# Six bound registers set once for 316 indirect transfers of GpSimd

## The chip, the core and the metric

The kernel runs on one core of a Trainium2 chip. A core has TensorE for matrix products (PE in the profile), VectorE (DVE), ScalarE (ACT), GpSimd (POOL) and SyncE (SP). Each engine has its own list of instructions; semaphores order them against each other. An engine has a sequencer in front of it, which works off the list; what the sequencer does by itself (set a register, wait on a semaphore, issue a DMA) stands in the profile under the engine's name with a q, as POOLq. The metric is the device time of one execution in microseconds. One execution was also recorded by the hardware profiler.

## The reference, cut to what matters

4096 tokens of width 128 pass through six layers. The first and third are a mixture of 8 experts, the fourth and sixth one of 16 experts with a limited capacity, the second is a convolution with attention-like cumulative products and a dense layer, and the fifth is a linear recurrence.

```
x = x + 0.5 * moe8(layernorm(x))                 # argmax of the scores chooses one of 8 experts per token
x = x + attn(layernorm(x))                       # conv, q/k/v, two cumulative sums, gelu layer
x = x + 0.5 * moe8(layernorm(x))
x = x + 0.5 * moe16(layernorm(x))                # one of 16 experts per token, at most 320 tokens each
x = x + recurrence(layernorm(x))                 # state = a * state + u_b, then layernorm
x = x + 0.5 * moe16(layernorm(x))
```

A mixture computes only the chosen expert, so tokens have to be brought together by expert and sent back to their places afterwards. That is what the indirect transfers do.

## The kernel before, in words

All tokens stay in the tile X: 32 tiles of 128 tokens, handled as 8 chunks of 4 tiles. Every engine works through an order written out by hand (TABLE), a list of steps with a number, and each step is one branch of that engine's program. Waits are on semaphores that count finished steps. A wait is attached to the instruction that follows it on its engine; where a step has several waits, instructions of their own (EVENT_SEMAPHORE, line 268) take all but the last.

The steps of GpSimd are these:

- `send.n` (line 1281) scatters tile n of X, whole rows of 132 numbers, to the DRAM array `xs`, to row numbers that VectorE has put into IDX. There are 128 of them, 32 for each mixture. In the 8-expert layers they come in groups (the first 8 or 20 tiles, then the rest), in the 16-expert layers one chunk after another. A group's first send waits for the array's fill and the row numbers in an instruction of its own, and then for `pnm`, which is VectorE's last step on the rows.
- `home.t` (line 1295) scatters the result tile `yt` of tile t of sorted tokens back to the tokens' places in the DRAM array `y`. There are 92, 46 for each 8-expert layer. It waits for `ty`, the step of VectorE that writes `yt`, and from the sixth on, in an instruction of its own, for the landing of the transfer five before.
- `ehome.i` (line 1310) does the same for one of the 16 experts in three blocks (128, 128 and 64 tokens), 96 transfers in all. The first and the third block wait for `eout`, VectorE's step at line 1065. In the last layer it writes to `out`, and its last block is the last work of the program.
- `ppow`, `apow`, `rpow` (lines 1261 and 1279) are small powers, 63 TENSOR_TENSOR instructions, for the layer norms.

SyncE loads sorted tiles (`tload`, line 500), experts' weights, and after the last `home` of a group the results (`yload`, line 515) back into X. The next layer needs them.

Each indirect transfer is issued through `send` (line 1263) or `home` (line 1267). Rows whose number is above a bound are dropped. The bound is given as a plain number, and the language then puts a register move (MOVE) ahead of the transfer; that MOVE is the instruction that follows the wait, so the step's last wait stands on it.

Of the kernel before, what the change touches and what calls it, by code (L numbers as in the profile page):

```python
# [14 lines left out]
P = 128  # L15
NT = 32
# [5 lines left out]
E0, E1 = 8, 16  # L22
# [8 lines left out]
ROOM = [T0[nt] for nt in GNT]  # L31
# [5 lines left out]
REACH = NT * P  # L37
# [242 lines left out]
def build(nc, x, consts, rows, cols, mats, xt, w01, w02, w1x, out):  # L280
    ctx = ExitStack()
    with ctx:
        sems = {}

        def sem(name):
            if name not in sems:
                sems[name] = ctx.enter_context(nc.semaphore("s_" + name))
            return sems[name]
# [10 lines left out]
        def dram(name, nrows, width):  # L299
            return nc.dram_tensor(name, (nrows, width), F32, kind="Internal").ap()  # L300
# [78 lines left out]
        xs0 = [dram(f"xs0_{g}", ROOM[g] * P, ROW) for g in range(4)]  # L379
        xs1 = [dram(f"xs1_{m}", E1 * REACH, ROW) for m in range(2)]  # L380
# [24 lines left out]
        def batch_x(b, col):  # L405

            c, n = BATCH[b][0] % NC, len(BATCH[b])
            return X[:, c * CT:(c + n) * CT, col]
# [29 lines left out]
        def wait_home(lane, t):  # L438
            lane.wait_ge(sem(f"home{t % NHS}"), turns(t, NHS))
# [15 lines left out]
        def filled0(g):  # L455
            return 32 if ROOM[g] >= ZR else 16
# [800 lines left out]
        def pool_program():  # L1257
            e = POOL.eng

            def power(dst, src):  # L1260
                return e.tensor_tensor(dst, src, MH[:, 0:dst.shape[1]], ALU.pow)  # L1261

            def send(dst, hi, n):
                return e.indirect_dma_start(dst, bass.IndirectOffsetOnAxis(ap=IDX[:, n:n + 1], axis=0), X[:, n, :], None,  # L1264
                                            bounds_check=hi, oob_is_err=False)

            def home(dst, src, ix):
                return e.indirect_dma_start(dst, bass.IndirectOffsetOnAxis(ap=ix, axis=0), src, None,  # L1268
                                            bounds_check=NT * P - 1, oob_is_err=False)

            e.memset(MH[:, :], -0.5).then_inc(sem("half"), 1)
            for b in PAD:
                e.memset(b[:, :, 0:3], 0.0).then_inc(sem("pad"), 1)
            POOL.wait_ge(sem("half"), 1)
            for stage, i in ORDER["pool"]:
                if stage == "ppow":
                    n = len(BATCH[i]) * CT
                    POOL.wait_ge(sem("peps"), i + 1)
                    e.tensor_tensor(batch_x(i, R_R), SMP[i % NSM][:, 0:n], MH[:, 0:n], ALU.pow).then_inc(sem("ppow"), 1)  # L1279
                elif stage == "send":  # L1280
                    p, n = divmod(i, NT)
                    c = n // CT
                    POOL.wait_ge(sem("pnm"), BOF[p * NC + c] + 1)
                    if p < 2:
                        g = 2 * p + (c >= FIRST[p])
                        POOL.wait_ge(sem("rsel"), 2 * (g + 1))
                        POOL.wait_ge(sem(f"fill{g}"), filled0(g))
                        send(xs0[g], ROOM[g] * P - 1, n).then_inc(sem(f"sent{g % 2}"), 16)
                    else:
                        k = (p - 2) * NC + c  # L1290
                        POOL.wait_ge(sem("q3"), 2 * (k + 1))
                        POOL.wait_ge(sem("q2"), 2 * (k + 1))
                        POOL.wait_ge(sem(f"fill{p + 2}"), 16 * E1)
                        send(xs1[p - 2], E1 * REACH - 1, n).then_inc(sem("sentx"), 16)
                elif stage == "home":
                    POOL.wait_ge(sem("ty"), i + 1)
                    if i >= NHS:
                        wait_home(POOL, i - NHS)
                    yt = YT[i % NYT]
                    home(y[i >= TILE0[2]], yt[:, :], XI[i % NXI][:, R_ID:ROW].bitcast(U32)).then_inc(sem(f"home{i % NHS}"), 16)  # L1300
                elif stage == "apow1":
                    POOL.wait_ge(sem("astat1"), 4 * (i + 1))
                    power(SMA[0][i % NA][:, 4:12], SMA[0][i % NA][:, 16:24]).then_inc(sem("apow1"), 1)
                elif stage == "apow2":
                    POOL.wait_ge(sem("astat2"), 3 * (i + 1))
                    power(SMA[1][i % NA][:, 4:8], SMA[1][i % NA][:, 16:20]).then_inc(sem("apow2"), 1)
                elif stage == "apow3":
                    POOL.wait_ge(sem("astat3"), 3 * (i + 1))
                    power(SMA[2][i % NA][:, 4:8], SMA[2][i % NA][:, 16:20]).then_inc(sem("apow3"), 1)
                elif stage == "ehome":  # L1310
                    xe, ye = XE[i % NXE], YE[i % NYE]
                    if i >= E1:
                        POOL.wait_ge(sem("out"), 16 * NC)
                    for b, (o, n) in enumerate(BL):
                        POOL.wait_ge(sem("eout"), 2 * i + (2 if b == 2 else 1))
                        home(y[1] if i < E1 else out, ye[0:n, b, :], xe[0:n, b, R_ID:ROW].bitcast(U32)).then_inc(sem(f"ye{i % NYE}"), 16)
                elif stage == "rpow":
                    POOL.wait_ge(sem("rstat"), 3 * (i + 1))
                    power(SMA[0][i % NA][:, 4:8], SMA[0][i % NA][:, 16:20]).then_inc(sem("rpow"), 1)
                elif stage == "rpow2":  # L1320
                    POOL.wait_ge(sem("rve"), i + 1)
                    power(SMA[1][i % NA][:, 4:8], SMA[1][i % NA][:, 16:20]).then_inc(sem("rpow2"), 1)
# [3 lines left out]
        dve_program()  # L1326
        act_program()
        pool_program()


# [60 lines left out]
```

## Time and profile before

| | before |
|---|---|
| median of 3 runs | 739.43 us (738.84 to 741.69) |
| the profiled execution | 738.26 us |
| its span, first to last instruction | 737.0 us |
| mean granted TensorE clock | 0.905 of full speed |
| PE, DVE, ACT, POOL busy | 81%, 59%, 45%, 53% of the span |

The span's stages: about 20 us of loading and routing, the first 8-expert layer to about 156 us, the second layer to about 256 us, the second 8-expert layer to about 420 us, the fourth layer with its 16 experts to about 550 us, the recurrence to about 640 us, and the last mixture of 16 experts to the end. In a profile a busy share is an average over such stages, and what a change is worth is read from the chain of waits in the stage where it acts. The chain goes back from the last instruction to whatever released each one.

### The profile page before, as it was taken

What the parts mean: (1) busy time and instruction counts of PE and PEld (TensorE: products, weight loads), DVE (VectorE), ACT (ScalarE), POOL (GpSimd) and SP (SyncE); (2) the same over time, 40 slices, a digit from 0 to 9 for tenths busy, and PEclk for the clock granted to TensorE, in tenths of its full rate; (3) what the DMA queues carried; (4) which work ended last, traced back from release to release, by engine and by line L of the source; (5) the groups of instructions that cost most, each with busy time, mean ns of one, the idle gap of its engine ahead of it and who ended that gap; (6) DMA issues with size and microseconds to landing.
All of it is one profiled execution on the core that took longest, in us unless ns stands there. A gap on an engine that the chain in (4) does not pass through costs nothing.

```text
span 737.0 us, 13471 instructions
## 1 busy us (share of the span) xinstructions
PE 597.7 (81%) x3640; PEld 487.9 (66%) x3640; DVE 433.2 (59%) x1670; ACT 332.0 (45%) x989; POOL 388.4 (53%) x386
## 2 busy tenths in 40 slices
PE   5568889988999967999999442999956866199996
PEld 5568889966757934899899341676734755066774
DVE  5554566569996687475568360455538897135453
ACT  1135366529577335445468532343306633334330
POOL 1667754446113185147757783355554488425555
PEclk9999899998999999999999855999986876599998
DMA  8676674660034222356684153377433122325410
GB/s 320 265 216 171 172 199 135 178 181 4 15 156 104 56 87 60 80 148 192 180 261 134 53 185 81 106 203 202 139 95 111 58 64 84 77 75 156 119 43 13
DMA packets 75257, 95.39 MB, mean 129 GB/s; under 512 B 12658, under 2 KB 51481, under 8 KB 74928
## 3 DMA queue, kind: packets, MB, share of 16 engines
q1 hardware_dynamic: 63664, 75.77, 35.4%
q0 software_dynamic: 10112, 14.55, 6.0%
q10 hardware_dynamic: 1408, 4.21, 1.7%
q8 instruction: 31, 0.51, 0.3%
q14 instruction: 42, 0.34, 0.1%
HBM read 66.24 MB, written 33.64 MB: 136 GB/s over the span
## 4 chain that ended last, share of the span: by engine, by line
PE 60%; DVE 11%; POOL 9%; issue 9%; DMA 8%; ACT 2%; SPq 0%; DVEq 0%; POOLq 0%; ACTq 0%
PE ps L704 10%; PE ps L639 9%; PE ps L711 9%; PE ps L631 9%; POOL xs L1264 6%; PE ps L686 3%; PE ps L679 3%; PE ps L588 3%; PE ps L549 3%; PE ps L653 3%; DMA X<-y 2%; PE ps L694 2%; DMA y<-yt,xi 2%; PE ps L718 2%; DMA xs<-X,IDX 1%
## 5 line engine op out<-in xcount | busy, mean ns | idle before, releaser
L1264 POOL DMA_INDIRECT xs<-X,IDX x128 | 128.0, 1000 | 51.1 <-issue 40.0
L1173 ACT ACTIVATE ht<-ps,CL 128x128 f32<-128x128 f32 x368 | 102.4, 378 | 91.2 <-PE ps L631 87.9
L1268 POOL DMA_INDIRECT y<-yt,xi x92 | 90.6, 984 | 61.8 <-DVE yt L957 40.7
L631 PE MATMUL ps<-xt,w1s 128*128 128x128 f32 x736 | 101.5, 288 | 11.8 <-DVE xt L951 8.0
L631 PEld LDWEIGHTS ps<-xt,w1s 128*128 128x128 f32 x736 | 93.1, 201 | 15.0 <-DVE xt L951 9.7
L639 PE MATMUL ps<-W,ht 128*128 x736 | 99.1, 282 | 1.2 <-ACT ht L1173 0.5
L639 PEld LDWEIGHTS ps<-W,ht 128*128 128x128 f32 x736 | 91.0, 195 | 5.7 <-issue 5.0
L1261 POOL TENSOR_TENSOR sma<-sma,MH 128x4 f32<-128x4 f32 (+1 forms) x40 | 48.1, 1207 | 79.3 <-DVE sma L749 63.7
L1230 ACT ACTIVATE hb<-ps 128x320 f32<-128x320 f32 x64 | 28.0, 437 | 73.5 <-PE ps L704 73.4
L1268 POOL DMA_INDIRECT y<-xu,x x36 | 34.3, 953 | 44.9 <-DVE xu L1065 34.9
L1053 DVE TENSOR_SCALAR hb<-ps 128x320 f32<-128x320 f32 x64 | 31.5, 492 | 41.3 <-PE ps L704 41.1
L1279 POOL TENSOR_TENSOR X<-smp,MH 128x4 f32<-128x4 f32 (+2 forms) x23 | 30.1, 1309 | 47.3 <-DVE smp L802 47.2
L957 DVE SCALAR_TENSOR_TENSOR yt<-ps,xb 128x128 f32<-128x128 f32 x92 | 26.6, 290 | 38.5 <-PE ps L639 31.7
L694 PE MATMUL ps<-KC,w1s 128*128 128x128 f32 (+1 forms) x96 | 20.6, 294 | 33.1 <-ACT w1s L1223 31.7
L1223 ACT ACTIVATE w1s<-x 128x128 f32<-128x128 f32 (+1 forms) x66 | 27.7, 483 | 39.3 <-DMA x<-xs 34.2
L937 DVE TENSOR_SCALAR xh<-xi 128x128 f32<-128x128 f32 x92 | 32.0, 355 | 19.0 <-DMA xi<-xs 11.5
L694 PEld LDWEIGHTS ps<-KC,w1s 128*128 128x128 f32 (+1 forms) x96 | 13.3, 147 | 43.3 <-ACT w1s L1223 33.7
L1058 DVE COPY ht<-ps 128x320 f32<-128x320 f32 x32 | 15.7, 492 | 44.0 <-PE ps L711 44.0
L711 PE MATMUL ps<-hb,W 128*128 128x320 f32 x136 | 40.3, 439 | 0.4 <-DVE hb L1053 0.3
L704 PE MATMUL ps<-ht,W 128*128 128x320 f32 x136 | 40.0, 433 | 0.0
L704 PE MATMUL ps<-ht,wx 128*128 128x320 f32 x120 | 39.2, 473 | 0.0
L1268 POOL DMA_INDIRECT out<-xu,x x30 | 28.6, 952 | 19.6 <-DVE xu L1065 12.6
(153 smaller groups left out, 1239.8 us busy)
## 6 DMA issues: line engine op xcount, KB each, us to landing
w1s<-in_w SPq DMA_DIRECT2D x92, 256.0 KB
W<-in_w1x SPq DMA_DIRECT2D x17, 512.0 KB, 3.9
wx<-in_w1x SPq DMA_DIRECT2D x15, 512.0 KB, 3.9
X<-y SPq DMA_DIRECT2D x24, 256.0 KB, 4.5
xi<-xs SPq DMA_DIRECT2D x92, 66.0 KB
xs<-ZB SPq DMA_DIRECT2D x32, 165.0 KB, 3.0
x<-xs SPq DMA_DIRECT2D x22, 132.0 KB, 2.3
X<-in_x SPq DMA_DIRECT2D x8, 264.0 KB, 8.8
```

The costliest lines, as they stand in the source:

```text
L631: r = e.matmul(ps[TILE_BANKS[i % n]][:, c * P:(c + 1) * P], W1[i % NW1][:, c * P:(c + 1) * P], XTT[i % NX][:, :], start=True, stop=True)
L639: r = e.matmul(ps[TILE_BANKS[i % len(TILE_BANKS)]][:, 0:P], HT[i % NHT][:, c, :], W02[:, bass.ds(r0 * F + c * P, P)], start=(c == 0), stop ...
L694: r = e.transpose(ps[0][:, o:o + n], EN[i % NEN][0:n, b, :], ident[0:n, 0:n])
L704: e.matmul(ps[2 + c][:, 0:CAP], WE[k % NW][:, c * P:(c + 1) * P], XET[k % NXET], start=True, stop=True).then_inc(sem("eup"), 1)
L711: r = e.matmul(ps[6 + i % 2][:, 0:CAP], WE[i % NW][:, F + c * P:F + (c + 1) * P], HB[i % 2][:, c, 0:CAP], start=(c == 0), stop=(c == 3))
L937: e.tensor_scalar(XH[i % NXH][:, :], xi[:, 0:P], xi[:, R_R:R_R + 1], xi[:, R_M:R_M + 1], ALU.mult, ALU.add).then_inc(sem("tn"), 1)
L1053: e.tensor_scalar(HB[k % 2][:, c, 0:CAP], ps[2 + c][:, 0:CAP], 0.0, None, ALU.max).then_inc(sem("erelv"), 1)
L1173: r = e.activation(HT[i % NHT][:, c, :], ps[TILE_BANKS[i % len(TILE_BANKS)]][:, c * P:(c + 1) * P], ACT.Gelu, bias=CL[:, bass.ds(r0 * 4 + ...
L1261: return e.tensor_tensor(dst, src, MH[:, 0:dst.shape[1]], ALU.pow)
L1264: return e.indirect_dma_start(dst, bass.IndirectOffsetOnAxis(ap=IDX[:, n:n + 1], axis=0), X[:, n, :], None, bounds_check=hi, oob_is_err=False)
L1268: return e.indirect_dma_start(dst, bass.IndirectOffsetOnAxis(ap=ix, axis=0), src, None, bounds_check=NT * P - 1, oob_is_err=False)
L1279: e.tensor_tensor(batch_x(i, R_R), SMP[i % NSM][:, 0:n], MH[:, 0:n], ALU.pow).then_inc(sem("ppow"), 1)
```

## The change

The helper `limit` allocates a register of GpSimd, moves a number into it and keeps it. At the start of GpSimd's program six of them are set: one for each of the four groups of the 8-expert layers, one for the 16-expert arrays, and one for the two `y` arrays and `out`. `send` and `home` pass the register as bound. Keeping a register copies it once, so that 12 MOVEs stand at the program's start. The 316 MOVEs ahead of the transfers are gone. A wait that stood on such a MOVE now stands on the transfer itself. The order of everything else is the same on all engines.

```diff
+            def limit(name, value):
+
+                r = nc.alloc_register(e.engine, name)
+                e.reg_mov(r, value)
+                return e.snap(r)
+
             def send(dst, hi, n):
                 return e.indirect_dma_start(dst, bass.IndirectOffsetOnAxis(ap=IDX[:, n:n + 1], axis=0), X[:, n, :], None,
                                             bounds_check=hi, oob_is_err=False)
 
             def home(dst, src, ix):
                 return e.indirect_dma_start(dst, bass.IndirectOffsetOnAxis(ap=ix, axis=0), src, None,
-                                            bounds_check=NT * P - 1, oob_is_err=False)
-
+                                            bounds_check=hi_home, oob_is_err=False)
+
+            hi_tile = [limit(f"hi_tile{g}", ROOM[g] * P - 1) for g in range(4)]
+            hi_expert = limit("hi_expert", E1 * REACH - 1)
+            hi_home = limit("hi_home", NT * P - 1)
...
-                        send(xs0[g], ROOM[g] * P - 1, n).then_inc(sem(f"sent{g % 2}"), 16)
+                        send(xs0[g], hi_tile[g], n).then_inc(sem(f"sent{g % 2}"), 16)
...
-                        send(xs1[p - 2], E1 * REACH - 1, n).then_inc(sem("sentx"), 16)
+                        send(xs1[p - 2], hi_expert, n).then_inc(sem("sentx"), 16)
```

## Rows read from the trace of the kernel before

**Rows 1.** The page's first part: busy us, share of the span, instructions.
```profile
PE 597.7 (81%) x3640; PEld 487.9 (66%) x3640; DVE 433.2 (59%) x1670; ACT 332.0 (45%) x989; POOL 388.4 (53%) x386
```

**Rows 2.** The chain that ended last, its shares by engine.
```profile
PE 60%; DVE 11%; POOL 9%; issue 9%; DMA 8%; ACT 2%; SPq 0%; DVEq 0%; POOLq 0%; ACTq 0%
```

**Rows 3.** Stretches: us, PE, PEld, DVE, ACT, POOL busy (count), clock, DMA share, GB/s.
```profile
330.00:372.00 42.00, 40.39 (x342) 38.46 (x341) 22.00 (x84) 22.32 (x80) 31.47 (x32) 1.00 0.65 188
...
420.00:452.00 32.00, 8.97 (x45) 7.85 (x45) 11.07 (x63) 5.61 (x27) 24.21 (x25) 0.50 0.42 137
452.00:550.00 98.00, 87.75 (x352) 60.41 (x352) 43.66 (x112) 34.02 (x80) 45.72 (x48) 0.94 0.53 150
```

**Rows 4.** Lines 1264 and 1268: the moves, ns min/median/max, first and last start.
```profile
L1264 POOLq MOVE  x128: 29/29/35, 20.4 to 630.8; - x128
...
L1268 POOLq MOVE  x188: 29/29/29, 55.0 to 732.7; - x188
```

**Rows 5.** The chain near the end of the program: start us, us, what.
```profile
727.13 0.61 DVE xu L1065 x2
...
727.77 0.03 POOLq L1268
...
728.31 0.03 POOLq L1268
...
728.53 0.36 POOL out L1268
```

**Rows 6.** The same chain where GpSimd's power waits for VectorE.
```profile
557.02 0.18 DVE sma L749
...
557.27 1.39 POOL sma L1261
```

**Rows 7.** GpSimd's timeline: start us, us, line, operation, [idle before, releaser].
```profile
69.28 0.97 POOL L1264 DMA_INDIRECT xs<-X,IDX  x1 [0.30 <-issue]
70.56 0.97 POOL L1268 DMA_INDIRECT y<-yt,xi  x1 [0.30 <-issue]
...
391.99 1.06 POOL L1279 TENSOR_TENSOR X<-smp,MH 128x4 f32<-128x4 f32 x1
393.23 1.04 POOL L1264 DMA_INDIRECT xs<-X,IDX  x1 [0.19 <-issue]
```

**Rows 8.** VectorE's timeline: what releases the power at 391.99.
```profile
391.12 0.16 DVE L802 TENSOR_SCALAR smp<-smp 128x4 f32<-128x4 f32 x1
```

**Rows 9.** The chain at the first send.
```profile
20.31 0.03 POOLq L268
20.34 0.04 issue
20.38 0.04 POOLq L1264
```

**Rows 10.** GpSimd's timeline where its two long unbroken stretches begin.
```profile
330.42 0.97 POOL L1268 DMA_INDIRECT y<-yt,xi  x1 [1.76 <-DVE IDX L872]
...
389.70 0.97 POOL L1268 DMA_INDIRECT y<-yt,xi  x1 [0.98 <-DVE yt L957]
```

**Rows 11.** The chain at the ends of those two stretches.
```profile
369.09 3.42 DMA y<-yt,xi
...
372.53 4.10 DMA X<-y
...
418.33 2.08 DMA y<-yt,xi
```

**Rows 12.** GpSimd's timeline at the last three blocks' first.
```profile
732.33 0.97 POOL L1268 DMA_INDIRECT out<-xu,x  x1 [0.33 <-issue]
```

**Rows 13.** Line 1268 from 330.43 to 370.1 us, and from 389.7 to 418.4 us.
```profile
L1268 POOL DMA_INDIRECT y<-yt,xi x19: 970/972/1090, 330.4 to 369.1; - x19
...
L1268 POOL DMA_INDIRECT y<-yt,xi x12: 966/971/1039, 389.7 to 418.3; - x12
```

**Rows 14.** The chain at the first 16-expert layer's start.
```profile
458.19 6.06 PE ps L704 x12
...
470.58 2.15 PE ps L704 x8
```

## The prediction

> **What bounds the kernel now.** I read the page first. PE is busy for 81% of the span and POOL for 53% [rows 1], so GpSimd is not the bound on average. In the chain of waits PE holds 60%, POOL 9% and POOLq less than half a percent [rows 2]: the moves themselves are hardly on the path, and what is to be found is the time around them. The table by stretches then shows where GpSimd matters. From 330 to 372 us it is busy for 31.5 of 42 us in 32 instructions, and from 420 to 452 us PE works for only 9 of 32 us while POOL works for 24 [rows 3]. The chain enters GpSimd at the sends (about 20 to 27, 257 to 289, 434 to 450 and 603 to 636 us) and at the last `home` or `ehome` of a group, whose landing releases the reload of X.
>
> Then I looked at one move closely. All 316 take 29 ns [rows 4]. At the end of the program VectorE finishes `xu` at 727.74; the MOVE starts at 727.77, the next MOVE at 728.31, the transfer at 728.53 [rows 5]. So from the release to the transfer's start 0.79 us pass, and the sequencer needs 728.31 − 727.80 = 0.51 us for one transfer behind its MOVE. Where GpSimd instead waits for VectorE with a power, which carries its wait itself, the power starts 0.07 us after the release [rows 6].
>
> Where transfers stand back to back, the moves run far ahead. The first `home` has its MOVE at 55.0 us [rows 4] and starts at 70.56 [rows 7], and still 0.30 us lie between it and the transfer before. That gap is therefore not the MOVE's; it belongs to the transfer. Behind a power it is 0.19 us [rows 7].
>
> **The change part by part.** *The moves' own time.* A MOVE fills 0.03 us and the pause ahead of it 0.04 us [rows 9], 0.07 us together. In an unbroken stretch, with one transfer each 0.97 + 0.30 = 1.27 us against 0.51 + 0.07 us of the sequencer, this is worth nothing: the cover is GpSimd's own work of 1.27 us. It is worth 0.07 us where a stretch starts after a wait that keeps an instruction of its own. Those are the first sends of the groups, at 20.4 us [rows 9] and, with the same pattern, at 39.1 and 256.3 us. They stand one after the other on the path: 3 x 0.07 = 0.2 us. The later groups of sends start while GpSimd is still busy with something else; I take nothing for them.
>
> *The 12 moves at the start.* 12 x 0.07 = 0.8 us of the sequencer, at a time when GpSimd waits for data to arrive and for VectorE: its first step on the chain is the send whose waits end at 20.3 us [rows 9]. So this is hidden; without that cover it would cost 0.8 us.
>
> *The wait that changes its place.* This is the larger term, and the trace has no indirect transfer that carries a wait. If the sequencer prepares the transfer before it waits, as the power's 0.07 us suggests that it does with a power, then of the 0.79 us only the 0.07 us of the power and the 0.19 us that a transfer starts later than a power remain: 0.26 us. The gain is 0.79 − 0.26 = 0.53 us for each start out of idleness. The bounds: if the transfer could start as early as a power, 0.72 us; if it is prepared only after the wait, the 0.07 us of the MOVE alone. I take 0.53, since the power is the nearest row of an instruction of this engine with a wait of its own.
>
> *How many of these starts are on the path.* Four.
> - At 330.42 a `home` starts after 1.76 us of idle time [rows 10], and from there to 370.1 GpSimd has no pause but the transfers' own: 31 transfers x 1.27 = 39.4 of 39.7 us (a 32nd instruction [rows 3] comes later). The last `home` before the reload starts at 369.09, lands at 372.5, and the reload releases VectorE and PE [rows 11]. Everything in the stretch moves with its start.
> - At 389.70 another starts after 0.98 us [rows 10], and the unbroken stretch from there ends in the `home` of 418.33, which releases the next reload [rows 11]. Within it stand powers that wait for VectorE. The first starts at 391.99 [rows 7] and was released at 391.12 + 0.16 = 391.28 [rows 8], so that 0.53 us fits; the two later ones have more room.
> - At the end of each 16-expert layer (546.35 and 732.33) the last three blocks come right behind the three before: 0.33 us of idle instead of 0.30 [rows 12]. So they depend as much on the start of the three before, 728.53 [rows 5], as on their own release, 732.33 − 0.79 = 731.54. The three before move to 728.00 and leave GpSimd free at 728.00 + 3 x 1.27 = 731.81; the release allows 731.54 + 0.26 = 731.80. Both move by 0.53, and so does the end.
>
> Elsewhere (homes from 95 to 156 and 292 to 330 us, `ehome` within the layers) the starts get earlier too, but the chain is on PE there, and nothing of it arrives at the end.
>
> Sum: 0.2 + 4 x 0.53 = 2.3 us. The profiled execution took 738.26 us (span 737.0), so it would take 736.0. It lies 1.2 us below the median of the runs, 739.43; from that the forecast is 737.1 us. With the bounds of the unknown cost the sum goes from 0.2 + 4 x 0.07 = 0.5 to 0.2 + 4 x 0.72 = 3.1 us.
>
> One rule bears on this term for the forecast. The Trainium skill, Perfetto Trace Analysis, section "DMA Instruction — SWDGE (GPSIMD)", lets the sequencer decode and push such a transfer first, and the semaphore wait comes after that in a queue; for a sequencer-only instruction the wait comes before its execution. No run here shows it yet; by that rule the sum stays 2.3 us.
>
> **The rivals.**
>
> *1. The transfer is prepared only after its wait.* Then the sequencer's 0.51 us stay behind the release and each of the seven starts gains the 0.07 us of the MOVE: 0.5 us, 738.9 us. For it: the 0.51 us is long against the 0.03 us of a MOVE, which shows that the sequencer has real work with a transfer, and a power needs no such work, so that its 0.07 us may say nothing here. Against it: nothing in the trace.
>
> The Trainium skill, DMA: Bandwidth & Descriptors, section "Anatomy of one DMA — SWDGE (gpsimd) path", says that any semaphore wait happens on the issuing sequencer before dispatch. It also gives about 50 ns for that dispatch, where this trace has 0.51 us [rows 5]; the measurement decides. By its rule on the wait the time is rival 1's.
>
> *2. A transfer with a wait no longer runs ahead, and the kernel gets slower.* Now the MOVE takes the wait, and the transfer behind it is prepared while GpSimd is busy with earlier ones. If a transfer that carries a wait were handed over only when GpSimd is free, its 0.51 us and the 0.19 us of its start would show in full in place of the 0.30 us gap, 0.40 us for each `home` in the unbroken stretches: 19 and 12 of them [rows 13], 31 x 0.40 = 12.4 us, 751.6 us with the 0.2 of the sends. It decides as soon as the gap is above the 0.30 + 2.3/31 = 0.37 us that would use up the gain. Against it: powers with a wait start without any gap behind a transfer (391.99 has none) [rows 7].
>
> *3. TensorE's clock.* At the start of the 16-expert layer a product of line 704 takes 6.06/12 = 0.51 us, later 2.15/8 = 0.27 us [rows 14], after a stretch at a granted clock of 0.50, that is 1.2 GHz, in which PE was mostly idle [rows 3]. If with shifted starts the clock rose later by another such dozen in both layers, 2 x 12 x 0.24 = 5.7 us would be lost, 742.8 us. Against it: the idle stretch ahead of it stays as long as it is.
>
> *4. The 0.30 us gap does hold the MOVE's 0.07 us.* Then all transfers of the GpSimd-bound stretches gain: 8, 24, 20, 31, 21, 13 and 21 of them by the timeline, 138 x 0.07 = 9.7 us more, 727.4 us. Against it stands the MOVE of 55.0 us for a transfer of 70.56 us [rows 4, 7]. That the change does less than it says is excluded: the moves are not in the program any more.
>
> **How the numbers follow.** Forecast 0.48, rival 1 0.28, rival 2 0.06, rival 3 0.06, rival 4 0.07, and 0.05 for effects of shifted transfers that I can't place. A measurement of this kernel tells 0.5% (3.7 us) from no change, that is below 735.7 or above 743.1. Forecast and rival 1 both lie within; of the forecast's chance I give 0.06 to faster, for its upper bound and the spread of the runs. Faster: 0.07 + 0.06 + 0.01 = 0.14. Slower: rival 2 with 0.06, a third of rival 3, and 0.01, together 0.09. Within: 0.77. The predicted time is 737.1 us. The range goes from 735.0 (the upper bound's 736.3 and the spread of the median, which was 0.6 us to the low side of three runs and 2.3 to the high side) to 741.0 us (rival 1 with the high side), and leaves out rivals 2, 3 and 4.
>
> **What would show each step.** In the profile after there are 12 moves, all before 3 us, and none on lines 1270 and 1274. The step on the wait is right if at the end a transfer starts about 0.26 us after `xu`, and wrong if it starts 0.7 us after it. The gap in unbroken stretches should stay at 0.30 us; at 0.23 rival 4 is right, at 0.7 rival 2. The stretches should start 0.5 us sooner after their `yt`. A difference in the first products of line 704 speaks for rival 3. I am wrong altogether if the span changes by more than 3.7 us while the starts after `yt` and `xu` do as I say.

## The result, and the profile after

The changed kernel takes 735.92 us in the median of 20 runs (732.42 to 739.79), and the kernel before, run in turn with it, 740.14 us (734.01 to 743.51, 20 runs). The ratio is 0.9951 with a 95% interval of 0.9931 to 0.9971: 3.6 us less, between 2.1 and 5.1. (The medians themselves differ by 4.2 us; all differences below are taken from the ratios on record, unless medians are named.) That is a small gain, but one that the interval holds away from nothing. The profiled execution took 737.36 us, with a span of 736.1 us at a granted clock of 0.906, against 738.26 and 737.0 us at 0.905 before.

The page's first part and the chain's shares, the counterparts of [rows 1] and [rows 2]:

```profile
PE 596.3 (81%) x3640; PEld 485.6 (66%) x3640; DVE 433.9 (59%) x1670; ACT 331.2 (45%) x989; POOL 390.4 (53%) x386
...
PE 59%; POOL 14%; DVE 12%; issue 7%; DMA 7%; ACT 1%; SPq 0%; DVEq 0%; ACTq 0%; POOLq 0%
```

No engine's busy time has moved by more than 2.3 us, and the counts are the same. GpSimd's share of the chain has grown from 9 to 14%. In part the chain now passes over the transfers themselves, where it went over the sequencer before ("issue" fell from 9 to 7%). In part it takes another way: from 39.5 to 68.7 us it runs over GpSimd's sends, where in the profile before it went over a load of `xi` (39.11 to 44.3 us) and, from 47 us on, over TensorE. So the two ways must lie near each other there. The three stretches of [rows 3] read as before too, to within 1.2 us of PE's busy time (columns as there):

```profile
330.00:372.00 42.00, 40.42 (x346) 38.78 (x345) 22.37 (x84) 22.11 (x80) 31.20 (x32) 1.00 0.67 192
420.00:452.00 32.00, 8.97 (x45) 7.85 (x45) 11.21 (x63) 5.61 (x27) 24.40 (x25) 0.50 0.42 137
452.00:550.00 98.00, 86.55 (x352) 59.72 (x352) 43.68 (x112) 33.74 (x80) 45.72 (x48) 0.94 0.54 150
```

Of the moves of [rows 4] only the twelve at the start are left, by the view of lines 1266 and 1267:

```profile
L1266 POOLq MOVE  x6: 29/29/35, 0.7 to 1.3; - x6
...
L1267 POOLq MOVE  x6: 34/34/38, 0.8 to 1.4; - x6
```

What has changed is the time from a release to the transfer. The chain near the end, where [rows 5] had two MOVEs:

```profile
730.53 0.02 issue
730.55 0.87 DVE xu L1065 x3
731.42 0.02 issue
731.44 0.97 POOL out L1274
732.41 0.30 issue
732.72 0.97 POOL out L1274
733.69 0.30 issue
733.99 0.91 POOL out L1274
```

The first of these transfers waits for the second of the three `xu`. Two took 0.61 us in [rows 5], so it was released at 730.55 + 0.61 = 731.16 and starts 0.28 us later, at 731.44. GpSimd was busy until 731.11, so this start lies close behind a transfer too. The three blocks before start out of idleness, and they are the counterpart of [rows 5]:

```profile
726.77 0.85 DVE L1065 SCALAR_TENSOR_TENSOR xu<-ps,x 128x128 f32<-128x128 f32 x3
...
727.64 0.97 POOL L1274 DMA_INDIRECT out<-xu,x  x1 [1.79 <-DVE xu L1065]
```

Again with 0.61 us for two, that is 727.64 − 727.38 = 0.26 us, where the kernel before took 728.53 − 727.74 = 0.79 us. The same at the head of the long stretch, first VectorE's `yt` and then GpSimd's timeline:

```profile
330.78 0.29 DVE L957 SCALAR_TENSOR_TENSOR yt<-ps,xb 128x128 f32<-128x128 f32 x1 [0.62 <-PE ps L639]
331.35 0.97 POOL L1274 DMA_INDIRECT y<-yt,xi  x1 [1.77 <-DVE rt_u L867]
332.63 0.97 POOL L1270 DMA_INDIRECT xs<-X,IDX  x1 [0.30 <-issue]
```

`yt` ends at 331.07, the transfer starts at 331.35: 0.28 us. In the kernel before `yt` ended at 329.36 + 0.29 = 329.65 and the transfer started at 330.42 [rows 10], 0.77 us later:

```profile
329.36 0.29 DVE L957 SCALAR_TENSOR_TENSOR yt<-ps,xb 128x128 f32<-128x128 f32 x1 [0.63 <-PE ps L639]
```

The second line also shows that the gap behind a transfer is still 0.30 us, as in [rows 7]. And the long stretch still takes the same time from its first `home` to its last: line 1274 in the window of [rows 13] runs from 331.4 to 370.0 us, 38.6 or 38.7 us as before.

```profile
L1274 POOL DMA_INDIRECT y<-yt,xi x19: 971/972/1101, 331.4 to 370.0; - x19
```

Note that the head of the stretch stands 0.9 us later in this profile (331.35 against 330.42), although its start came 0.5 us sooner after `yt`. Single executions differ by some 4 us at this place for other reasons: in a kernel further down, with the same start behind `yt`, the stretch begins at 327.39 us. So the pair of profiles shows how one start works, and the medians what it is worth.

### The profile page after: what moved, and what is told of

The parts are those of the page before. It is cut to its first block, busy times and chain, and to the rows that moved or that the text cites. A ratio compares the mean times of both kernels' runs of the same rounds, so it can differ in the third digit from the quotient of the medians.

```text
span 736.1 us, 13167 instructions
## 1 busy us (share of the span) xinstructions
PE 596.3 (81%) x3640; PEld 485.6 (66%) x3640; DVE 433.9 (59%) x1670; ACT 331.2 (45%) x989; POOL 390.4 (53%) x386
## 4 chain that ended last, share of the span: by engine, by line
PE 59%; POOL 14%; DVE 12%; issue 7%; DMA 7%; ACT 1%; SPq 0%; DVEq 0%; ACTq 0%; POOLq 0%
PE ps L704 10%; POOL xs L1270 10%; PE ps L711 10%; PE ps L639 8%; PE ps L631 8%; PE ps L588 4%; PE ps L686 3%; PE ps L679 3%; PE ps L653 3%; PE ps L549 3%; PE ps L694 2%; DMA X<-y 2%; PE ps L718 2%; POOL sma L1261 1%; POOL y L1274 1%
## 5 line engine op out<-in xcount | busy, mean ns | idle before, releaser
L1274 POOL DMA_INDIRECT y<-yt,xi x92 | 91.9, 999 | 56.7 <-DVE yt L957 38.4
L1223 ACT ACTIVATE w1s<-x 128x128 f32<-128x128 f32 (+1 forms) x66 | 27.7, 483 | 38.4 <-DMA x<-xs 31.0
L704 PE MATMUL ps<-ht,W 128*128 128x320 f32 x136 | 40.4, 437 | 0.0
```

Source lines behind the costliest of these rows:

```text
L704: e.matmul(ps[2 + c][:, 0:CAP], WE[k % NW][:, c * P:(c + 1) * P], XET[k % NXET], start=True, stop=True).then_inc(sem("eup"), 1)
```

## The experiments

The theory after the result: a transfer that carries its own wait is prepared (decoded and made ready, the 0.51 us between two MOVEs in [rows 5]) by GpSimd's sequencer while it waits, a MOVE between wait and transfer keeps that preparation behind the release, and this 0.5 us is all that the change gains. The rivals: the moves' own number and time; a side effect of shifted transfers; and, for the size, that the shift counts at other places than the four.

Four kernels ran in a first series, in which the kernel before took 738.91 us (35 runs).

**Moves ahead of the waits.** All 316 moves are back, and each stands ahead of its step's waits.

```diff
-                r = nc.alloc_register(e.engine, name)
-                e.reg_mov(r, value)
-                return e.snap(r)
+                return nc.alloc_register(e.engine, name), value
+
+            def fresh(hi):
+                e.reg_mov(hi[0], hi[1])
+                return hi[0]
...
+                    fresh(hi_home)
                     POOL.wait_ge(sem("ty"), i + 1)
```

> All 316 moves are back, but each stands ahead of its step's waits, and the wait stays on the transfer. Theory A (the gain comes from the place of the wait: a transfer with its own wait is prepared ahead of it): the transfer starts about 0.28 us after yt, as in the changed kernel (before: 0.77), and the time is that of the changed kernel, ratio to before 0.995 (0.993 to 0.997). Theory B (the gain comes from the moves' own sequencer time, 316 x 0.07 us, wherever they stand): the start after yt is 0.28 or 0.77, but the ratio is 1.000.

Measured: 735.62 us, ratio 0.9956 (0.9929 to 0.9983). Line 1268, then `yt` and the transfer at the head of the stretch:

```profile
L1268 POOLq MOVE  x316: 29/29/35, 10.3 to 732.9; - x158
...
326.82 0.29 DVE L957 SCALAR_TENSOR_TENSOR yt<-ps,xb 128x128 f32<-128x128 f32 x1 [0.62 <-PE ps L639]
...
327.39 0.97 POOL L1276 DMA_INDIRECT y<-yt,xi  x1 [1.77 <-DVE rt_u L867]
```

With as many moves as before, the transfer starts 327.39 − 327.11 = 0.28 us after `yt`, and the kernel is as fast as the changed one. The number of moves is worth nothing that these runs can measure.

**Moves behind the waits.** The same six registers, each set again directly ahead of the transfer:

```diff
-                                            bounds_check=hi, oob_is_err=False)
+                                            bounds_check=fresh(hi), oob_is_err=False)
```

> Six registers as in the change, but each is set again directly ahead of each transfer, behind the step's wait, so that the wait stands on the move again. Theory A: start after yt 0.77 us, ratio to before 1.000 (within 0.002). Theory B: also 1.000, since the moves are back. Theory C (what helps is that six registers are used instead of one fresh register for each transfer): 0.995.

Measured: 738.70 us, ratio 0.9995 (0.9967 to 1.0022).

```profile
331.82 0.29 DVE L957 SCALAR_TENSOR_TENSOR yt<-ps,xb 128x128 f32<-128x128 f32 x1 [0.63 <-PE ps L639]
...
332.88 0.98 POOL L1276 DMA_INDIRECT y<-yt,xi  x1 [1.75 <-DVE IDX L872]
```

Here it is 332.88 − 332.11 = 0.77 us, as before the change. The two kernels differ only in the side of the wait on which a move stands, and by 0.9995 − 0.9956 = 0.0039 of 738.91 us, 2.9 us, give or take 2.8 (the two intervals taken together). The interval just excludes zero. With the moves behind the waits nothing of the change's gain shows any more, although the registers are there.

**Six more semaphore instructions at the homes.** This is the kernel of moves behind the waits, and `home` has in addition thirteen waits that have long been met, which become six instructions (line 1270) between the MOVE and the transfer:

```diff
+                for k in range(more):
+                    e.wait_ge(sem("half"), 1)
...
+                                            bounds_check=fresh(hi_home, 13), oob_is_err=False)
```

> The kernel before with six more sequencer instructions (waits that are long satisfied) between the move and the transfer of home and ehome, about 0.5 us: every start of such a transfer out of idleness comes 0.5 us later than before, the mirror image of the change. The sequencer then needs about 1.1 us for a transfer, still below the 1.27 us of GpSimd. With four such starts on the path: +2.0 us, ratio 1.003. With seven (which the measured gain of 3.6 us would need at 0.5 us each): +3.6 us, ratio 1.005. If the place of the starts did not matter at all (the gain had another cause): 1.000.

Measured: 739.67 us, ratio 1.0017 (0.9990 to 1.0043). The chain before the last transfer:

```profile
735.80 0.62 DVE xu L1065 x2
...
738.99 0.04 POOLq L1270
739.04 0.09 POOL out L1278
739.12 1.16 issue
740.28 0.91 POOL out L1278
```

From the last `xu`'s group to the last transfer's start it is 740.28 − 735.80 = 4.48 us, against 3.44 in the changed kernel (733.99 − 730.55). So a start is later by about 1.0 us than in the changed kernel and 0.5 than before, and the medians go the same way: 0.0061 over the moves ahead of the waits, 4.5 us, where four starts on the path of 1.0 us each would make 4. Against the kernel before, and against the moves behind the waits (0.0022, 1.6 us, give or take 2.8), the loss is not clear of nothing; the expectation was 2.0 us.

**The last wait stands on the send.** In the changed kernel the send's own wait is `pnm`, which is met early; the wait for the row numbers, which is met last, stands in an instruction of its own ahead of it. Of a step's waits the one written first stands on its instruction. So `pnm` goes behind, for the 16-expert layers as well:

```diff
                 elif stage == "send":
...
-                    POOL.wait_ge(sem("pnm"), BOF[p * NC + c] + 1)
...
                         POOL.wait_ge(sem("rsel"), 2 * (g + 1))
+                        POOL.wait_ge(sem("pnm"), BOF[p * NC + c] + 1)
```

> The changed kernel, with the order of waits of send turned round, so that the wait that ends last (rsel for a group of the 8-expert layers, q3 for the 16-expert layers) stands on the transfer and the early ones in instructions of their own. Theory A: the first send of a group starts about 0.3 us after VectorE's row numbers instead of 0.8, 0.5 us sooner at 21, 39.5 and 258 us, all three on the path, 1.5 us or 0.2% below the changed kernel, ratio to before 0.993. If these starts are covered: 0.995.

Measured: 734.99 us, ratio 0.9955 (0.9923 to 0.9987). The chain at the first send, of the changed kernel:

```profile
19.89 0.28 DVE IDX L872
20.17 0.03 POOLq L268
20.20 0.83 issue
21.04 1.17 POOL xs L1270
```

and of this one:

```profile
19.41 0.28 DVE IDX L872
19.69 0.29 issue
19.98 1.17 POOL xs L1270
```

0.87 us from the release to the transfer have become 0.29: a semaphore instruction between the wait and the transfer holds its preparation up just as a MOVE does. The three first sends start 0.58, 0.48 and 0.48 us sooner behind their IDX than in the changed kernel (0.29, 0.27 and 0.29 us against 0.87, 0.75 and 0.77). The expectation was 0.993 if all three are on the path and 0.995 if they are covered; 0.9955 is that of the moves ahead of the waits, so in this series the half microseconds are not seen in the time.

A second series was to say at which starts the half microsecond counts. The changed kernel was given late starts, by 1.0 us, at one group of places at a time, with the MOVE and the six semaphore instructions from above:

```diff
+            def home(dst, src, ix, late=False):
+                if late:
+                    e.reg_mov(hi_late, NT * P - 1)
+                    for k in range(13):
+                        e.wait_ge(sem("half"), 1)
...
-                    home(y[i >= TILE0[2]], yt[:, :], XI[i % NXI][:, R_ID:ROW].bitcast(U32)).then_inc(sem(f"home{i % NHS}"), 16)
+                    home(y[i >= TILE0[2]], yt[:, :], XI[i % NXI][:, R_ID:ROW].bitcast(U32), i < 54).then_inc(sem(f"home{i % NHS}"), 16)
```

In this series the kernel before took 785.39 us (780.2 to 789.48, 35 runs), 6% more than in the two others; ratios are formed within it.

**Late homes 0 to 53.**

> The changed kernel, but home.0 to home.53 (the first 8-expert layer and the first eight of the second) again have a move behind their wait, and six long satisfied waits in instructions of their own behind it: these transfers start about 1.0 us later after yt than in the changed kernel (0.5 us later than before). The prediction holds that PE covers all of them: ratio to before as the changed kernel, 0.995. If they carry the part of the gain that the sum lacked (3.6 measured against 2.3), the time goes up by twice that part, 2.6 us: 0.999.

Measured: 784.59 us, ratio 0.9990 (0.9957 to 1.0022).

**Late homes 54 to 91** (`i >= 54`).

> The same delay of about 1.0 us only for home.54 to home.91 of the second 8-expert layer. By the prediction's count two such starts (330 and 390 us) lie on the path: 2 x 1.0 us over the changed kernel, ratio to before 0.998. If PE covers them too: 0.995. If more than two of them count, four or more: 1.000 and above.

Measured: 783.48 us, ratio 0.9977 (0.9946 to 1.0009).

**Late ehomes** (all 96 blocks instead of the homes).

> The same delay of about 1.0 us only for the 96 ehome transfers. By the prediction's count the ends of the two 16-expert layers take it over in full: the time from the last xu to the end grows from 4.65 to 5.7 us, 2 x 1.0 us over the changed kernel, ratio to before 0.998. If the first of the two is covered by something: 0.9965. If neither counts beyond that: 0.995.

Measured: 786.53 us, ratio 1.0015 (0.9986 to 1.0044).

**The changed kernel again**, without an edit.

> The changed kernel once more, beside the three above on the same chip. Ratio to before 0.995 again (0.993 to 0.997) if the measured gain stands; nearer 0.997 if the first measurement was on the high side of what the sum of 2.3 us allows.

Measured: 781.62 us, ratio 0.9961 (0.9934 to 0.9988). Against it the three groups cost 0.0029, 0.0016 and 0.0054 (2.3, 1.3 and 4.2 us), each with an uncertainty of about 0.004. Only the last stands clear. The first group's 0.9990 is what was expected if those homes do count, against 0.995 by the prediction's count, but the uncertainty covers both. Which homes count cannot be read from this.

A third series repeated it with fewer, larger groups. The kernel before was back at 741.03 us (29 runs), although the record names the same chip (4) for the second and the third series.

**The last wait on the send, again.**

> The version with the last wait of send on the transfer, once more and beside the changed kernel on one chip. Its three group starts came 0.5 us sooner in the profile; if they are all on the path it lies 1.5 us, 0.2%, below the changed kernel (0.993 against 0.995). If not, both have the same ratio.

Measured: 734.84 us (6 runs), ratio 0.9911 (0.9877 to 0.9946).

**The changed kernel again.**

> The changed kernel as reference for the three beside it: 0.9955 (0.993 to 0.998).

Measured: 737.42 us, ratio 0.9952 (0.9925 to 0.9979), the third value of this kernel within 0.001 of the others.

**Late ehomes again.** (The "other chip" of this expectation is the second series.)

> The changed kernel with the 96 ehome transfers 1.0 us later. On the other chip it was 4.2 us above the changed kernel, where the two ends of layers account for 2.1 us. If the ends are all, it is 2.1 us above here, ratio 0.998. If transfers within the layers count as well, 4 us or more: 1.001.

Measured: 740.01 us, ratio 0.9982 (0.9958 to 1.0005), 0.0030 or 2.2 us over the changed kernel, give or take 2.6. The end of its chain is the one of the six semaphore instructions:

```profile
736.31 0.62 DVE xu L1065 x2
...
739.63 1.16 issue
740.79 0.91 POOL out L1278
```

**Late homes, all 92.**

> The changed kernel with all 92 home transfers 1.0 us later. By the prediction's count two of their starts are on the path, 2.0 us above the changed kernel, ratio 0.998. If PE covers all: 0.9955. If the homes of the first 8-expert layer count as well (a third start, at the end of its first and second group): 0.9995.

Measured: 740.60 us, ratio 0.9970 (0.9940 to 1.0000), 0.0018 or 1.3 us over the changed kernel, give or take 3. The medians, 740.60 against 737.42 us, lie 3.2 us apart; so loosely is this cost known. Its head of the stretch, GpSimd's and VectorE's timeline:

```profile
330.97 0.29 DVE L957 SCALAR_TENSOR_TENSOR yt<-ps,xb 128x128 f32<-128x128 f32 x1 [0.62 <-PE ps L639]
332.56 0.97 POOL L1278 DMA_INDIRECT y<-yt,xi  x1 [1.78 <-DVE yt L957]
333.83 0.97 POOL L1270 DMA_INDIRECT xs<-X,IDX  x1 [0.31 <-issue]
```

332.56 − 331.26 = 1.30 us, 1.0 more than in the changed kernel, and the gap after it is 0.31 us. The delay moves the stretch as a whole and does not add up in it.

## Why the prediction was right, point by point

**The 12 moves at the start** are hidden, as said. All stand before 1.5 us. GpSimd's own first work, a `memset`, moves from 0.73 to 1.47 us, but then GpSimd waits for VectorE, and its first power starts at 9.94 us as it did at 10.06 before. (In [rows 4] most of the moves take 29 ns and some up to 35, not all 29 as the prediction has it; nothing hangs on it.)

**The sends' 0.07 us, three times.** From the end of IDX to the first send it was 21.25 − 20.31 = 0.94 us in the kernel before ([rows 9], and the row of its chain below) and is 0.87 now. At the other two it was 0.83 and 0.85 and is 0.75 and 0.77. The size is right. That all three are on the path is not: in the profile before, the chain does not contain the send of 39.83 us and goes over the load of `xi` at 39.11 and TensorE; in the profile after it passes over the send at 39.54.

```profile
21.25 0.31 POOL xs L1264
```

It could have been 0.56 to 0.65 us per send, by the kernel with the last wait on the send: the change left the last wait in an instruction of its own and so kept the preparation behind it. The prediction did not ask for that, though it is the same mechanism.

**The wait that changes its place.** Forecast 0.26 us from the release to the start, measured 0.28; forecast gain 0.53 us, measured 0.49 to 0.53 (0.77 to 0.28 at `yt`, 0.79 to 0.26 and 0.28 at `xu`). That the moves ahead of the waits start their transfers as early as no moves, and the moves behind them as late as before, shows that what stands between wait and transfer is the cause. That it works through the preparation rests on the 0.51 us between two MOVEs, which is the size of the shift; the MOVE itself starts 0.03 us after the release [rows 5], so the release is not noticed late. Rival 1, with 0.7 us from the release to the start, is out. The Trainium skill, Perfetto Trace Analysis, section "DMA Instruction — SWDGE (GPSIMD)", has the sequencer decode and push such a transfer before its wait; these runs agree, with 0.28 us against 0.77 us. The rule of the Trainium skill, DMA: Bandwidth & Descriptors, section "Anatomy of one DMA — SWDGE (gpsimd) path", by which the wait comes on the sequencer before dispatch, does not fit the transfers here that carry their own wait: they start 0.28 us after it, which leaves no room for 0.51 us.

**Four starts on the path.** The ends of the two 16-expert layers behave as worked out; the last one is shown here. The last group of `xu` starts at 730.93 and the last transfer at 734.88 in the kernel before, 3.95 us, and 3.44 in the changed one: the end has moved by 0.51. That is GpSimd's timeline of before, behind [rows 12], and VectorE's:

```profile
730.93 0.86 DVE L1065 SCALAR_TENSOR_TENSOR xu<-ps,x 128x128 f32<-128x128 f32 x3 [0.64 <-PE ps L718]
...
734.88 0.91 POOL L1268 DMA_INDIRECT out<-xu,x  x1 [0.30 <-issue]
```

Two layer ends, later by 1.0 us each, should cost 2.0 us; the late ehomes cost 2.2 in the third series and 4.2 in the second. The two starts of homes should cost 2.0 us together and cost 1.3. With 2.6 and 3 us of uncertainty none of these is shown by the times; they only do not contradict the count.

The homes' two starts are the weaker half of it. The chain passes through neither of them, before or after: from 334 to 353 us it goes over TensorE, and it reaches GpSimd's stretch only late, at 356.30 before and 366.19 after; from 390 to 408 us it is mostly on TensorE too. GpSimd's timeline is unbroken, so that the last `home` can't come sooner than the first one allows, but TensorE, busy for 40.4 of 42 us [rows 3], runs beside it in nearly the same time. That an earlier start arrives at the end in full was argued, and no run shows it. The start at 389.70 us can moreover not gain its 0.53 us. In the profile after it does not come out of idleness:

```profile
388.51 1.03 POOL L1270 DMA_INDIRECT xs<-X,IDX  x1 [0.20 <-issue]
389.85 0.98 POOL L1274 DMA_INDIRECT y<-yt,xi  x1 [0.30 <-issue]
```

The `home` stands at the usual 0.30 us behind a send, where 0.98 us of idle time were before [rows 10]. With an early start the transfer in front sets the time. The same holds in three other profiles with prepared transfers: the start comes 0.48 us behind its `yt` here, 0.61 with the moves ahead of the waits, 0.49 with the last wait on the send and 0.49 in the changed kernel of the third series, each time 0.30 us behind the send, against 0.77 in the kernel before. So this start gains 0.2 to 0.3 us, and not 0.53.

**Rivals 2 and 4** needed another gap in the unbroken stretches, above 0.37 or 0.23 us; it is 0.30. **Rival 3**: the first dozen products of line 704 take 4.85 us, less than the 6.06 of [rows 14], and the later eight the same 2.15:

```profile
458.58 4.85 PE ps L704 x12
...
469.76 2.15 PE ps L704 x8
```

The clock was granted as before, 0.50 in the stretch ahead and 0.94 in the layer. In the last layer it is the other way round: from its first products of line 704 to the group of two at 651.97 us (652.35 before) 9.11 us pass, 0.96 more than before. Both look like scatter between executions: the first dozen takes 4.62 us with the moves behind the waits and 4.58 to 5.35 in the four further profiles without late starts (both kernels with the last wait on the send, the moves ahead of the waits, the changed kernel again), and the second span 8.30 us and 8.07 to 9.07.

**The size.** The forecast was 2.3 us; 3.6 were measured, between 2.1 and 5.1. Halving the costs of the late starts (1.0 us against 0.5) gives 1.1 us for the ehomes and 0.7 for the homes, with the sends' 0.2 together 2.0 us. Neither this nor the forecast is excluded by the one measurement. The four values of the kernels with prepared transfers, 0.9951, 0.9956, 0.9961 and 0.9952, make 3.3 us in the mean, with an uncertainty of about 0.9 if they are taken as independent, an estimate. The forecast lies at the edge of that, and with 0.2 to 0.3 us for the start at 389.70 its sum would be about 2.0 us. So about 1 us may come from starts that the prediction counted at nothing, such as the homes before the 54th (2.3 us for a start 1.0 us later, with an uncertainty of some 3; but all 92 together cost no more than 1.3). So the mechanism and the size of one shift are as forecast; that the sum comes near is in part luck, because one start was put too high and something else was left out. What else it was stays open.

**A better version.** The changed kernel with the last wait on the send may be better still: 0.9955 and 0.9911 of the kernel before. In the third series that is 0.0041, 3.0 us, under the changed kernel, with 6 runs and an uncertainty of 3.3; in the first series it is level with the moves ahead of the waits. The three earlier starts explain 1.5 us at most. That it is faster than the changed kernel is not shown.

## What to carry to other kernels

When an engine waits for another and then issues an indirect transfer, look at what stands between the wait and the transfer on its sequencer. In this kernel a register move or a semaphore instruction there cost not its own 0.03 us but the whole preparation of the transfer, 0.5 us, at every start out of idleness; so set registers ahead of the wait, and let the transfer itself carry the wait that is met last. Then count only the starts that begin an unbroken stretch or end the program: inside a stretch the preparation was hidden behind the transfer before. And ask of each such start whether something else in front of it, as the send at 388.51 us here, or another engine beside the stretch takes the gain back.

## What the runs showed of the hardware that was not expected

The preparation can be moved away, but the transfer's own gap can't: 0.30 us lie between two transfers in a stretch with a move for each [rows 7] and without any, and 0.30 or 0.31 with six more semaphore instructions ahead of each (the last three transfers of that kernel, 0.97 us long, start at 737.73, 739.00 and 740.28 us).

In the second series every kernel was some 6% slower (785.39 us for the kernel before, 781.62 for the changed one), and the ratio between them stayed the same, 0.9961 against 0.9951 and 0.9952. The waits of the changed kernel in that series show where the time went, with columns engine, line, waited for, us, times, longest:

```profile
POOL y L1274 <- DVE yt L957: 82.5, 57, 4.3
ACT ht L1173 <- remote: 38.7, 4, 25.8
DVE yt L957 <- remote: 21.3, 2, 14.1
```

GpSimd waited 82.5 us for `yt` where it waited 38.4 in the profile after (the row below), and single waits of the 8-expert layers on something outside the traced engines lasted up to 25.8 us.

```profile
POOL y L1274 <- DVE yt L957: 38.4, 36, 3.6
```

TensorE was busy for 12 us more than in the profile after, of 44 us more in the span (780.2):

```profile
PE 608.2 (78%) x3640; PEld 495.3 (63%) x3640; DVE 433.9 (56%) x1670; ACT 332.6 (43%) x989; POOL 391.0 (50%) x386
```

What held these layers up isn't shown by the trace, and no kernel was made to find it. Only kernels of one series can be compared, and what the late groups cost in the second series was measured on an execution whose 8-expert layers waited elsewhere.
